# Shifted tiles loaded from 256-byte boundaries, in a displaced Gaussian convolution followed by a Hadamard mix

## The reference

```python
x = x + _L0_conv_ref(_gn(x), L0_conv_offset)   # displaced 3x3 depthwise Gaussian
x = x + _L1_conv_ref(_gn(x))                   # Hadamard over channels
...
# _L0: 48 offsets, 8 channels each; off_int = round(64 * offset)
iy = jnp.arange(h)[None, :] - dy[:, None]
ix = jnp.arange(w)[None, :] - dx[:, None]
shifted = x[:, ch, iyc, ixc] * mask            # zero outside the image
out = depthwise_conv3x3(shifted, gaussian(64 * offset - off_int))
# _L1: pad 384 channels to 512, multiply by the 512x512 Hadamard, keep 384
```

## Time and profile before

| | us |
|---|---|
| median of 3 runs | 257.6 (256.43 to 259.06) |
| profiled execution, time | 258.49 |
| profiled execution, span | 256.7 |
| DVE busy | 197.5 (77%) |
| PE busy | 163.9 (64%) |
| ACT busy | 136.2 (53%) |
| POOL busy | 38.7 (15%) |

### The profile page before, as it was taken

One profiled execution on the slowest core, in us unless ns is written; L12 is line 12 of the kernel. 1 busy time (PEld: TensorE's weight loads), 2 busy tenths in 40 slices (PEclk: granted clock), 3 DMA queues, 4 the chain that ended last, 5 costly groups with the idle time before them and its releaser, 6 DMA issues.

```text
span 256.7 us, 2406 instructions
## 1 busy us (share of the span) xinstructions
PE 163.9 (64%) x664; PEld 94.4 (37%) x664; DVE 197.5 (77%) x321; ACT 136.2 (53%) x217; POOL 38.7 (15%) x39
## 2 busy tenths in 40 slices
PE   0000000607986969758896696999999999989610
PEld 0000000407735639658853422444433333333200
DVE  0799999999973179855850348999999999999930
ACT  1000999679762056315210499898887877870000
POOL 0000000000000052100104782000705370000000
PEclk9999999999996599997999577999999999999965
DMA  5999999999999308999971657239999999997798
GB/s 166 416 411 409 409 409 290 363 410 409 409 306 258 80 2 235 337 273 279 269 169 22 173 189 259 84 92 368 349 325 412 402 416 406 403 410 320 278 407 344
DMA packets 26223, 76.79 MB, mean 299 GB/s; under 512 B 7969, under 2 KB 8225, under 8 KB 25921
## 3 DMA queue, kind: packets, MB, share of 16 engines
q1 hardware_dynamic: 19616, 67.12, 71.9%
q0 software_dynamic: 4752, 9.45, 12.0%
q10 hardware_dynamic: 1840, 0.06, 0.5%
HBM read 67.07 MB, written 29.99 MB: 378 GB/s over the span
## 4 chain that ended last, share of the span: by engine, by line
DVE 39%; DMA 33%; SPq 10%; PE 7%; ACT 3%; issue 2%; ACTq 0%; DVEq 0%
DMA ring<-x_pad 27%; DVE ring L959 21%; DVE parts L273 10%; PE ps L570 3%; DMA blk<-x_pad 3%; SPq L291 2%; PE ps L659 2%; SPq L310 2%; SPq L292 2%; DMA stat_rows<-blk_stat 2%; ACT blk L534 2%; DVE blk L273 2%; PE ps L589 1%; ACT parts L542 1%; SPq L303 1%
## 5 line engine op out<-in xcount | busy, mean ns | idle before, releaser
L659 PE MATMUL ps<-parts,had_sb 128*128 128x512 f16 x216 | 55.1, 391 | 8.0 <-DVE parts L273 5.7
L959 DVE SCALAR_TENSOR_TENSOR ring<-ps,beta,ring 128x1024 f32<-128x1024 f32 x48 | 59.8, 1280 | 0.4 <-PE ps L659 0.4
L579 PE MATMUL ps<-geo_sb,blk 128*128 128x128 f32 x72 | 12.0, 320 | 51.9 <-DMA blk<-x_pad 45.4
L823 DVE BATCH_NORM_STATS2 halfstat<-ring 128x6 f32<-128x512 f32 x64 | 38.8, 673 | 1.9 <-DMA ring<-x_pad 1.8
L589 PE MATMUL ps<-parts 128*128 128x160 f32 (+2 forms) x180 | 31.2, 336 | 11.8 <-ACT parts L464 10.2
L534 ACT ACTIVATE blk<-ring,gn 128x1024 f32<-128x1024 f32 x32 | 37.8, 1227 | 0.0
L273 DVE TENSOR_TENSOR parts<-blk,parts 128x1024 f16<-128x1024 f32 x27 | 32.9, 1219 | 6.0 <-ACT parts L542 6.0
L285 POOL DMA_INDIRECT ring<-x_rows,row_at x24 | 29.7, 1237 | 50.8 <-DMA ring<-x_pad 38.5
L659 PEld LDWEIGHTS ps<-parts,had_sb 128*128 128x128 f16 x216 | 20.4, 100 | 44.2 <-issue 11.2
L589 PEld LDWEIGHTS ps<-parts 128*128 128x128 f32 x180 | 29.8, 214 | 13.1 <-ACT parts L464 10.6
L669 PE MATMUL ps<-ring,first_w 128*128 128x512 f32 x64 | 32.3, 628 | 0.0
(11 more groups left out here) (117 smaller groups left out, 146.6 us busy)
## 6 DMA issues: line engine op xcount, KB each, us to landing
ring<-x_pad SPq DMA_DIRECT2D x20, 1536.0 KB, 15.3
out<-ring SPq DMA_DIRECT2D x13, 1536.0 KB, 7.4
blk<-x_pad SPq DMA_DIRECT2D x15, 512.0 KB, 17.1
out<-ring SPq DMA_DIRECT2D x9, 512.0 KB, 5.1
x_rows<-blk POOLq DMA_DIRECT2D x6, 512.0 KB, 6.9
other_a<-x_pad SPq DMA_DIRECT2D x2, 512.0 KB, 8.3
x_rows<-other_a POOLq DMA_DIRECT2D x2, 512.0 KB, 6.1
geo_sb<-geo SPq DMA_DIRECT2D x1, 683.0 KB, 4.8
```

Source lines behind the costliest of these rows:

```text
L579: last = pe.transpose(pixels[:, j // 4, 128 * (j % 4):128 * (j % 4 + 1)], shifted[:, 128 * j:128 * (j + 1)], eye)
L659: last = pe.matmul(ps[n % 4][:, h, :], had_sb[:, sign, :], part_of(n, t, part)[:, 512 * h:512 * (h + 1)], start=False, stop=ends and part ...
L823: last = dve.bn_stats(halfstat[:, i % 4, t, h, :], ring[:, t, place_of(i), 512 * h:512 * (h + 1)])
L959: dve.scalar_tensor_tensor(ring[:, m, place_of(i), :], ps[n % 4][:, :, :].rearrange("p a n -> p (a n)"), beta[:, i % BATCH:i % BATCH + 1], ...
```

## The change

The host now lays the channels 1088 elements apart (`PITCH`), 1024 pixels and 64 zeros (`GRAIN`), where they were 1024 apart. The address of a shifted tile is split on the chip: its multiple of 64 elements (256 bytes) below it, and a remainder of 0 to 63 elements, which goes into a fourth column of `place`. The shifted load starts at the multiple and brings 1088 elements for each partition in place of 1024. ACT loads the remainder into a register and reads the tile from that column on: in `centre`, which it does anyway, and, for slots 0 and 1, in a new copy after image 9, on which PE's transposes now wait (`settled`). DVE's chain ahead of `place` has four more small operations. The plain loads, the image loads and the reloads take 1024 of each 1088 elements. To make room, `off_sb` and `moment` move into other tiles. The rare branch gets the same treatment.

```diff
+GRAIN = 64
+PITCH = PIXELS + GRAIN
...
-    x_bcp = x_pad[:, PIXELS:PIXELS + CHANNELS * PIXELS].rearrange("b (t c n) -> b c t n", t=CT, c=128)
+    x_bcp = x_pad[:, PITCH:PITCH + CHANNELS * PITCH].rearrange("b (t c n) -> b c t n", t=CT, c=128)[:, :, :, 0:PIXELS]
...
-        blk = sb("blk", [128, 2 * DEEP, PIXELS])
+        blk_room = sb("blk_room", [128, DEEP * (PIXELS + PITCH)])
+        blk = blk_room[:, 0:2 * DEEP * PIXELS].rearrange("p (u n) -> p u n", n=PIXELS)
+        shifted = blk_room[:, DEEP * PIXELS:].rearrange("p (u n) -> p u n", n=PITCH)
...
                 if k >= DEEP:
                     sp.wait_ge(flipped, k - DEEP + 1)
-                sp.dma_start(blk[:, DEEP + k % DEEP, :],
-                             x_pad[:, ds(at, BIND * PIXELS)].rearrange("b (c n) -> b c n", c=BIND)).then_inc(shift_in[k % DEEP], 16)
+                sp.dma_start(shifted[:, k % DEEP, :],
+                             x_pad[:, ds(at, BIND * PITCH)].rearrange("b (c n) -> b c n", c=BIND)).then_inc(shift_in[k % DEEP], 16)
...
                 sp.dma_start(own_x[k % WIDE],
-                             x_pad[:, ds(at, BIND * PIXELS)].rearrange("b (c n) -> b c n", c=BIND)).then_inc(x_in[k % WIDE], 16)
+                             x_pad[:, ds(at, BIND * PITCH)].rearrange("b (c n) -> b c n", c=BIND)[:, :, 0:PIXELS]).then_inc(x_in[k % WIDE], 16)
...
+                if i == EARLY_FLIP - 1:
+                    act.wait_ge(place_done, 1)
+                    for k in range(EARLY):
+                        skip = act.value_load(place[0:1, k, 3:4], min_val=0, max_val=GRAIN - 1)
+                        act.wait_ge(shift_in[k], 16)
+                        act.activation(shifted[:, k, 0:PIXELS], shifted[:, k, ds(skip, PIXELS)], ACT.Copy).then_inc(settled, 1)
...
                 act.wait_ge(gn_in[k], 16)
-                act.activation(blk[:, DEEP + u, :], blk[:, DEEP + u, :], ACT.Identity,
+                skip = act.value_load(place[0:1, k, 3:4], min_val=0, max_val=GRAIN - 1)
+                act.activation(shifted[:, u, 0:PIXELS], shifted[:, u, ds(skip, PIXELS)], ACT.Identity,
                                bias=blk_gn[:, k, 0:1], scale=1.0).then_inc(centred, 1)
...
                 if k < EARLY:
-                    pe.wait_ge(shift_in[k], 16)
+                    pe.wait_ge(settled, k + 1)
...
-                link(dve.tensor_tensor(place_f[:, keep, 2:3], place_f[:, keep, 2:3], place_f[:, keep, 1:2], ALU.add))
+                link(dve.tensor_tensor(place_f[:, keep, 3:4], place_f[:, keep, 2:3], place_f[:, keep, 1:2], ALU.add))
+                link(dve.tensor_scalar(place_f[:, keep, 2:3], place_f[:, keep, 3:4], 1.0 / GRAIN, 0.5 / GRAIN - 0.5, ALU.mult, ALU.add))
+                link(dve.tensor_scalar(place_f[:, keep, 2:3], place_f[:, keep, 2:3], ROUND, None, ALU.add))
+                link(dve.tensor_scalar(place_f[:, keep, 2:3], place_f[:, keep, 2:3], ROUND, float(GRAIN), ALU.subtract, ALU.mult))
+                link(dve.tensor_tensor(place_f[:, keep, 3:4], place_f[:, keep, 3:4], place_f[:, keep, 2:3], ALU.subtract))
                 dve.tensor_copy(place[:, keep, :], place_f[:, keep, :]).then_inc(placed, 1)
...
-    x_pad = np.zeros((BATCH, (CHANNELS + 2) * PIXELS), x.dtype)
-    x_pad[:, PIXELS:PIXELS * (CHANNELS + 1)] = x.reshape(BATCH, -1)
+    x_pad = np.zeros((BATCH, CHANNELS + 2, PITCH), x.dtype)
+    x_pad[:, 1:CHANNELS + 1, 0:PIXELS] = x.reshape(BATCH, CHANNELS, PIXELS)
```

More of the change, by code:

```diff
@@ L39 @@
 TAPS_X, TAPS_Y = WIDTH, 6
-MORE_LINKS = 33
+MORE_LINKS = 37
 CHUNKS = 8
@@ L173, in build @@
         spare += 6 * OFFSETS
+        off_sb = early[:, spare:spare + 2 * OFFSETS]
         taps = early[:, spare:spare + FAST * 44].rearrange("p (k d) -> p k d", k=FAST)
         spare += FAST * 44
-        place_f = early[:, spare:spare + FAST * 3].rearrange("p (k d) -> p k d", k=FAST)
+        place_f = early[:, spare:spare + FAST * 4].rearrange("p (k d) -> p k d", k=FAST)
         axes = EARLY * 2
@@ L216, in build @@
         upper_masked = sem("upper_masked")
+        settled = sem("settled")
         convolved = sem("convolved")
@@ L357, in _ @@
                     c_at = sp.value_load(place[0:1, 0, 0:1], min_val=0, max_val=CHANNELS - BIND)
-                    x_at = sp.value_load(place[0:1, 0, 1:2], min_val=PIXELS, max_val=PIXELS * (CHANNELS - BIND + 1))
-                    s_at = sp.value_load(place[0:1, 0, 2:3], min_val=1, max_val=PIXELS * (CHANNELS - BIND + 2) - 1)
-                    sp.dma_start(blk[:, 0, :], x_pad[:, ds(x_at, BIND * PIXELS)].rearrange("b (c n) -> b c n", c=BIND)).then_inc(more_in, 16)
-                    sp.dma_start(blk[:, DEEP, :], x_pad[:, ds(s_at, BIND * PIXELS)].rearrange("b (c n) -> b c n", c=BIND)).then_inc(more_in, 16)
+                    x_at = sp.value_load(place[0:1, 0, 1:2], min_val=PITCH, max_val=PITCH * (CHANNELS - BIND + 1))
+                    s_at = sp.value_load(place[0:1, 0, 2:3], min_val=GRAIN, max_val=PITCH * (CHANNELS - BIND + 1) + PIXELS - GRAIN)
+                    sp.dma_start(blk[:, 0, :], x_pad[:, ds(x_at, BIND * PITCH)].rearrange("b (c n) -> b c n", c=BIND)[:, :, 0:PIXELS]).then_inc(more_in, 16)
+                    sp.dma_start(shifted[:, 0, :], x_pad[:, ds(s_at, BIND * PITCH)].rearrange("b (c n) -> b c n", c=BIND)).then_inc(more_in, 16)
                     sp.dma_start(blk_gn[:, 0, :], gn_rows[ds(c_at, BIND), :].rearrange("c (b k) -> b c k", k=2)).then_inc(more_in, 16)
@@ L514, in _ @@
                     act.wait_ge(more_in, 48 * m + 48)
-                    act.activation(blk[:, DEEP, :], blk[:, DEEP, :], ACT.Identity,
+                    act.activation(pivot[:, 0:1], pivot[:, 0:1], ACT.Copy)
+                    skip = act.value_load(place[0:1, 0, 3:4], min_val=0, max_val=GRAIN - 1)
+                    act.activation(shifted[:, 0, 0:PIXELS], shifted[:, 0, ds(skip, PIXELS)], ACT.Identity,
                                    bias=blk_gn[:, 0, 0:1], scale=1.0).then_inc(more_centred, 1)
@@ L575, in _, with transpose_block @@
             eye = geo_sb[:, G_EYE:G_EYE + 128]
-            def transpose_block(pixels, shifted):
+            def transpose_block(pixels, tile):
                 for j in range(CHUNKS):
                     last = pe.transpose(pixels[:, j // 4, 128 * (j % 4):128 * (j % 4 + 1)],
-                                        shifted[:, 128 * j:128 * (j + 1)], eye)
+                                        tile[:, 128 * j:128 * (j + 1)], eye)
                 return last
@@ L602, in transposes @@
                     pe.wait_ge(upper_masked, k - 1 - EARLY)
-                transpose_block(ps[k % 2], blk[:, DEEP + k % DEEP, :]).then_inc(flipped, 1)
+                transpose_block(ps[k % 2], shifted[:, k % DEEP, :]).then_inc(flipped, 1)
             def convolve(k):
@@ L642, in _ @@
                     pe.wait_ge(more_centred, m + 1)
-                    transpose_block(ps[0], blk[:, DEEP, :]).then_inc(more_flipped, 1)
+                    transpose_block(ps[0], shifted[:, 0, :]).then_inc(more_flipped, 1)
                     pe.wait_ge(more_masked, m + 1)
```

12 lines of the change are left out of this document (6 added, 6 removed).

## The result

The changed kernel is slower: median 260.74 us (257.18 to 265.69, 22 runs) against 256.48 (254.28 to 259.06, 22 runs), ratio 1.013, 95% interval 1.0098 to 1.0164. Ratios leave out a kernel's runs more than 1.5% above its fastest; the medians of all runs stand at 1.017 here. The forecast was 253.8, in a range of 251.4 to 257.7, so its sign and its range were both missed. It took 3.8 off 257.6, the median of the three runs known then; the 22 runs of before put that at 256.48.

A forecast was written before the change was run, and what follows sets the result against it. It took DMA to bound the statistics stage and hold up the block stage, DVE the Hadamard stage. Gains of 1.0 (statistics) and 2.9 (block) sum to 3.9, giving a median of 253.8 us, range 251.4 to 257.7.

The forecast's parts named there:

- Is the start address the cause?: Shifted loads: eight of nine start off a 64-element boundary, taken as why each costs twice its bytes in DMA time.
- The excess of 1.4 us a load: Shifted loads: each costs 2.7 us of all DMA engines, 1.4 us more than its bytes need.
- The rule that I set against the rows: Shifted loads: skill's 256-byte-piece arithmetic, 130 beats against 128, only 2% slow; the prediction went by the profile's factor of two.
- the address isn't the cause: Rival, 9%: something else slows the shifted loads, none gets faster and they carry 1/16 more bytes; 258.1 us.
- The statistics stage: Stage up to the last image's statistics: gain 1.0 us, the last image landing earlier until DVE becomes the end of the wait.
- DVE's 0.8: Statistics stage: four more chained DVE operations cost 0.8 us, covered by its 1.83 us idle before the last image.
- The block stage: Stage of the tile slots: gain 2.9 us, range 0 to 4.5, from faster shifted loads less ACT's exposed register load.
- The 3.9 of the loads: Block stage: three off-boundary shifted loads give back 4.2 us, less 0.3 for added bytes, so 3.9 us.
- ACT's exposed register load: Block stage, in `centre`: behind the waits, not hidden; takes some 0.7 us off each tile's gain for slots 6 to 8.
- ACT's register loads join the chain: Rival, 7%: block-stage centring comes 1.1 us late for slots 5 to 8, losing 4.4 us; 261.0 us.
- The first rival's doubt: Rival, 22%: block-stage gain small, held by SP's issue order, stores sharing engines or ACT's register loads; 256.3 us.
- The rival of the pitch: Rival, 3%: the host's new pitch slows every load, statistics stage ends some 30 us later; 287 us or so.

The follow-up runs named there:

- e3: Kernel before with every shifted tile loaded from its plain tile's address, on a 256-byte boundary, the shift left out of the result; ratio to before 1.0023.
- e4: Kernel before with every shifted tile loaded from 128 consecutive channels of one image, 28 bytes off a 256-byte boundary (wrong data); ratio to before 0.9949.
- e13: Kernel before with the host's data ordered channel, image, pixel, so that every tile is 128 even rows; ratio to before 1.0028.
- e14: The changed kernel run once more, for a second profile; ratio to the kernel before 1.0197.
- e12: Kernel before plus ACT's two early copies, in place, with PE's early transposes waiting for them; ratio to before 0.9934.
- e2: Changed kernel with shifted loads of 1024 elements from their exact addresses, remainder 0, ACT's and DVE's added instructions kept; ratio to before 1.0119.
- e6: Kernel before with ACT's and DVE's part of the change alone, host layout and transfers as before, remainder 0; ratio to before 1.0133.
- e11: Kernel before plus an unused ACT register load before each of seven centrings, behind their waits; ratio to before 1.0032.
- e17: Changed kernel with POOL's stores cut to 128 of 1024 pixels, the rest filled after the last slot; block stage 35.9 us, from 44.2.
- e18: Kernel before with POOL's stores cut to 128 of 1024 pixels, the rest filled after the last slot; block stage 34.2 us, from 40.7.
- e5: Kernel before with unused elements behind each image on the host, images 1,679,872 bytes apart as in the changed kernel; ratio to before 1.001.
- e7: Kernel before with the images on the host exactly 2 MiB apart; ratio to before 1.0098.
- e8: Kernel before with each image on the host 1280 bytes farther from the one before it; ratio to before 0.9944.
- e9: Kernel before with shifted tiles from one image as 16 groups of 8 channels, one channel left out between groups (wrong data); ratio to before 0.9979.
- e10: Kernel before with block tiles in the order 8 channels outside, 16 images inside, for tiles, means and stores; ratio to before 1.120.

## Why the prediction was wrong

**The step that failed is "Is the start address the cause?"** It was answered from eight of nine offsets that lay off the boundary, a correlation. e3 and e4 turn it round: aligned 249 GB/s, unaligned 408. What the runs showed in its place is the form of the transfer: 16 groups of 8 rows load slowly wherever they start, and the change kept that form. The profile of before could have said so. "The plain and image loads, all on it, are fast" was wrong for the plain ones. The shifted tile of slot 4, the last of three, issued at 62.5, landed after 18.5 us at 81.0, and three plain ones were still to land. Windows of before behind that point:

```profile
82.00:84.50 2.50, 2.16 (x11) 2.16 (x11) 0.25 (x2) 0.00 (x0) 0.00 (x0) 0.50 1.02 251
81.00:84.00 3.00, 1.97 (x10) 1.87 (x9) 0.83 (x4) 0.00 (x0) 0.00 (x0) 0.50 1.06 265
```

The plain tiles alone, on the boundary, ran at 251 to 265 GB/s at a full share, no faster than the shifted ones. The stretch from 76 to 83 had put both under the name of the shifted loads.

**The excess of 1.4 us a load** was real, and measured right: e4 and e13 win 2.8 us on the image load caught behind two of them (17.9 for 20.7), where I had 2 x 1.4. DVE then starts on the last image at 72.9 and 73.2 without a wait, as the 73.02 read from the earlier trace rows said. Only the cause was wrong, so the change won nothing of it.

**The rule that I set against the rows** was right. By the Trainium skill (DMA: Bandwidth & Descriptors, "How a descriptor splits into AXI transactions") a start off the boundary costs the beats of the unused bytes before it, 2% by the prediction's count. e4 agrees with it, with 408 GB/s off the boundary, and so does e3, with 249 on it. The rival "the address isn't the cause" had the mechanism; at 9% it was priced far too low, and its 258.1 missed the rest of the loss.

**The statistics stage**: gain 1.0 forecast, loss 1.0 measured. DVE's 0.8 were covered as said: in e14 DVE still waited 1.61 us for the last image. ACT's copies cost nothing, as said; e12 even gains. The last image came later because the image loads did, which I had at their old time but for bytes: the pitch costs them 1 us in sum.

**The block stage**: gain 2.9 forecast, loss 3.4 measured. The 3.9 of the loads did not come. ACT's exposed register load of some 0.7 a tile was about right (0.6), and the mechanism of the rival "ACT's register loads join the chain" (7%, 261.0) is what e2, e6 and e11 show, with 1 us for the stage rather than 4.4. That its 261.0 lies beside the measured 260.74 is luck. The 3.4 took the long rows as well (44.2 against 42.0 for e2), and the meeting with the stores, as far as e17 and e18 show it; no part of the prediction had that, and the longer rows were booked by their bytes (0.3 us).

**The first rival's doubt**, "by stores that share the engines", was sound: e18 takes 6.5 us off the stage by cutting them. A form that is fast by itself did not shorten the stage: e4's shifted tiles leave it at 39.9 us and all of e13's at 41.2, within or just above the scatter. So in these two the 2.9 would not have come even with the right cause. What loads that stay fast beside the stores would give isn't shown, as e13's weren't.

**The rival of the pitch** (every load half as fast, 287) did not occur: image loads by themselves still move 408 GB/s.

**Open.** Why rows in the form 16 by 8 load at 250 GB/s: the profile doesn't tell the DMA engines apart. The Trainium skill (DMA: Bandwidth & Descriptors, "The descriptor swizzle") has each engine write the partitions of one port in a transfer to 128 partitions; whether the two-level form breaks this up no run here shows. Open, too, how the stores' meeting with long rows and late centring costs the other 1.7 us, and why e13's even tiles land so late beside the stores.

## What to carry to other kernels

Before a slow transfer is put down to one of its properties, look in the same trace for a transfer that shares all but that one; a window in which only the other kind is in flight would have done here. Write a transfer's rows as one even list, not as groups with gaps, where the load runs by itself or beside other loads, and don't leave 8 as its outermost dimension. Look at the stores before expecting the whole kernel to gain. A DMA share of 1 says that the engines hold packets, not that the stage waits for bytes: cut or speed up one kind of transfer before counting on its gain.

## What the runs showed of the hardware

- With tiles of 128 rows of 4 KB in flight the rate is 408 to 410 GB/s where they are one even list (e4, e13), and 237 to 249 with image loads beside them (41 to 46 in before, e3, e5, e7, e8, e9) or 251 to 265 by themselves (before) where they are 16 groups of 8, at every alignment and image distance tried. In mean time of a packet, 16 engines x 4096 bytes by 409 and 247 GB/s, that is an estimate of 160 against some 265 ns.
- Beside POOL's stores the even list isn't fast: plain tiles of e13 issued from 99 to 112 landed after 10.9 to 12.8 us, those of before after 6.6 to 8.4.
- The same 128 rows as 8 groups of 16, by themselves, keep the DMA engines half busy (share 0.52, 174 GB/s, e10).
- Gaps of 256 bytes between rows of 4096 bytes, never read, cost the image loads about 1 us in all, with their rate by themselves unchanged at 408 to 409.
- A register load of ACT behind a wait opens 0.6 us where the load is listed with 0.28.
- Two copies of ACT put in ahead of PE's early transposes made the kernel 0.7% faster (e12, 0.989 to 0.998).
